# Value products of two attention steps in one block behind the scores of the even step, with a ring of 12 tiles of exponentials

## The reference

```python
q = (h @ Wq.T + bq).reshape(B, S, nh, hd)      # nh = 16, hd = 16, S = 2048
k = (h @ Wk.T + bk).reshape(B, S, nh, hd)
v = (h @ Wv.T + bv).reshape(B, S, nh, hd)
scores = jnp.einsum('bqhd,bkhd->bhqk', q, k) * scale
scores = jnp.where(causal, scores, jnp.finfo(scores.dtype).min)
attn = jax.nn.softmax(scores, axis=-1)
o = jnp.einsum('bhqk,bkhd->bqhd', attn, v).reshape(B, S, H)
return o @ Wo.T + bo
```

## Time and profile before

| what | value |
|---|---|
| median of 3 runs | 1266.43 us |
| profiled execution | 1264.95 us |
| its span | 1263.2 us |
| TensorE busy | 1106.1 us, 88% |
| VectorE busy | 705.4 us, 56% |
| ScalarE busy | 562.9 us, 45% |
| GpSimd busy | 110.1 us, 9% |
| exponentials L955 | 298.0 us, 640 of them |
| value products L894 | 158.2 us, 1280 records |

### The profile page before, as it was taken

The page is one execution under the profiler, slowest core; times in us unless marked ns, Lnnn a source line. Parts: engine busy times, 40 slices in busy tenths (PEclk is TensorE's granted clock), DMA queues, the critical chain, the costliest instruction groups (busy, mean ns, idle before and its releaser), DMA issues. The chain is left out here.

```text
span 1263.2 us, 19302 instructions
## 1 busy us (share of the span) xinstructions
PE 1106.1 (88%) x6480; PEld 719.7 (57%) x6480; DVE 705.4 (56%) x1604; ACT 562.9 (45%) x1102; POOL 110.1 (9%) x409
## 2 busy tenths in 40 slices
PE   3289999999968267888999999999966999999998
PEld 2178888888856022333333333333226888888886
DVE  7923333334367375776988888888516233333333
ACT  6422222222247024665577777777762232223222
POOL 0000000000000112332211111111121000000000
PEclk9999999999989558999999999999987999999999
DMA  5000000000027402112111101110000000000000
GB/s 172 1 1 1 1 1 1 0 0 0 0 65 181 105 23 61 50 50 70 27 44 47 43 24 36 40 47 2 1 13 1 1 1 17 1 17 0 17 0 17
DMA packets 69243, 37.24 MB, mean 29 GB/s; under 512 B 47409, under 2 KB 63025, under 8 KB 69169
## 3 DMA queue, kind: packets, MB, share of 16 engines
q1 hardware_dynamic: 69168, 36.32, 10.7%
HBM read 25.63 MB, written 10.49 MB: 29 GB/s over the span
## 5 line engine op out<-in xcount | busy, mean ns | idle before, releaser
L955 ACT ACTIVATE attn_prob<-psum 128x512 f32<-128x512 f32 (+3 forms) x640 | 298.0, 541 | 157.8 <-PE psum L858 157.0
L294 PE MATMUL psum<-ffn_xt,all_w_hi 128*128 128x512 f32 x1024 | 325.5, 399 | 4.9 <-DVE ffn_xt L375 4.9
L978 DVE TENSOR_REDUCE attn_part_max<-psum 128x1 f32<-128x512 f32 x384 | 242.2, 684 | 61.5 <-PE psum L870 60.1
L381 DVE TENSOR_TENSOR ffn_inner<-ffn_act_out,ffn_inner 128x512 fp32r<-128x512 f32 x128 | 88.6, 692 | 331.4 <-ACT ffn_inner L345 331.4
L870 PE MATMUL psum<-attn_k_st,attn_q_st 96*128 96x512 bf16 (+3 forms) x640 | 222.7, 366 | 50.2 <-DMA attn_vals<-v_rows 30.9
L353 ACT ACTIVATE ffn_act_out<-psum 128x512 f32<-128x512 f32 x128 | 76.5, 598 | 370.9 <-PE psum L294 370.8
L858 PE MATMUL psum<-attn_q_st,attn_k_st 99*128 99x512 bf16 (+3 forms) x640 | 219.9, 359 | 9.3 <-ACT attn_prob L955 5.2
L294 PEld LDWEIGHTS psum<-ffn_xt,all_w_hi 128*128 128x128 f32 x1024 | 185.1, 190 | 43.5 <-issue 5.7
L308 PE MATMUL psum<-all_w_hi,ffn_inner 128*128 128x256 f32 x1024 | 202.9, 281 | 4.1 <-DVE ffn_inner L381 4.1
L294 PE MATMUL psum<-ffn_xt,all_w_lo 128*128 128x512 f32 x512 | 203.5, 398 | 0.0
L308 PEld LDWEIGHTS psum<-all_w_hi,ffn_inner 128*128 128x128 f32 x1024 | 165.3, 188 | 10.8 <-DVE ffn_inner L381 5.7
(11 more groups left out here) (97 smaller groups left out, 666.0 us busy)
## 6 DMA issues: line engine op xcount, KB each, us to landing
qk_parts<-qkv_parts SPq DMA_DIRECT2D x16, 384.0 KB, 2.6
attn_q_st<-qk_parts SPq DMA_DIRECT2D x32, 96.0 KB
attn_k_st<-qk_parts SPq DMA_DIRECT2D x16, 192.0 KB
all_x<-in_L_attn_h SPq DMA_DIRECT2D x4, 512.0 KB, 7.5
v_rows<-qkv_rows_v SPq DMA_DIRECT2D x16, 128.0 KB, 3.4
attn_q_st<-qk_parts SPq DMA_DIRECT2D x32, 64.0 KB
attn_k_st<-qk_parts SPq DMA_DIRECT2D x32, 64.0 KB
attn_k_st<-qk_parts SPq DMA_DIRECT2D x16, 128.0 KB
```

The costliest lines, as they stand in the source:

```text
L294: last = nc.tensor.matmul(psum[:, 2 * m + q % 2, :], w_part[a][:, 3 * g + m, pl, o:o + P], xt[:, k, c, pl, :], start=(n == 0), stop=(n == 5))
L381: nc.vector.tensor_tensor(inner[:, 1, u, :], act_out[:, u, :], as_f32(inner[:, 0, u, :]), ALU.subtract).then_inc(s["inner_lo"], 1)
L955: nc.scalar.activation(prob[:, n % PRING, at:BT], psum[:, S0 + n % SBANKS, at:BT], ACT.Exp).then_inc(s["exp"], 1)
L978: nc.vector.tensor_reduce(to, psum[:, bank, :], AX.X, ALU.max).then_inc(s["max_read"], 1)
```

## The change

The value products of steps d - 2 and d - 1 are issued together behind the scores of an even step d; behind an odd step there are none. At the end the products of the last two steps follow. The ring of exponentials has 12 tiles, three steps, instead of 8, and ScalarE waits for the products of step d - 3 where it waited for those of step d - 2.

```diff
-PRING = 8
+PRING = 12
...
                             for g in turned(d):
                                 turn_max(g)
-                            if d >= 1:
+                            if d >= 2 and d % 2 == 0:
+                                weigh(d - 2)
                                 weigh(d - 1)
+                        weigh(NS - 2)
                         weigh(NS - 1)
                         gather(NG_A - 1)
...
                         for d, (g, kb) in enumerate(steps):
-                            if d >= 2:
-                                act.wait_ge(s["weighted"], d - 1)
+                            if d >= 3:
+                                act.wait_ge(s["weighted"], d - 2)
```

## The result

| | before | after |
|---|---|---|
| median | 1265.20 us (4 runs) | 1284.16 us (4 runs, 1282.05 to 1287.15) |
| profiled execution | 1264.95 us | 1284.92 us |
| span | 1263.2 us | 1283.2 us |

The ratio of after to before is 1.0152, 95% interval 1.0122 to 1.0182: 19 us slower. The forecast was 1280 us in a range of 1268 to 1291. In the changed source the lines from L926 on lie two lower: the exponentials are L957, the reads of the maxima L980 and L983, the copies L938 and L944. L858, L870 and L894 keep their numbers.

The account below looks back on a forecast made before the run. Three engines were taken as nearly level, held together by three score and three maximum banks. Terms 13.0 + 0.9 + 2 - 2 + 0 = +13.9 us on 1264.95 gave 1278.9, stated as 1280 us, range 1268 to 1291.

Parts of the forecast that it names:

- the cycle: Repeating 14 steps of query blocks 2 and 3 for a pair of heads: from 38.96 to 40.8 us.
- The saving at the joint: Two value runs in a row on TensorE: a pair costs 0.24 us less than two single runs.
- The starved readers: VectorE and ScalarE late once a pair: +1.86 us a cycle, +13.0 us over steps 49 to 146; chance 0.67.
- the last twelve: Steps 148 to 159, without maxima: two or three full pairs of 5.23 against 4.90 us, +0.9 us.
- Steps 12 to 35: Waits for masks shrink by 3.4 us, starvation adds 1.2: together -2 us, bounds -4 and +3.
- the wait for the masks: Steps 12 to 35: value products wait 1.0 us for POOL four times; 0.15 us remains of each, -3.4 us.
- Steps 37 to 48 and 1 to 6: Six maxima a step in steps 36 to 48: +2 us, bounds 0 and +4; first twelve steps: 0, bounds -1 and +1.
- a DMA that is waited for can swallow part of it: Steps 36 to 48: a DMA wait ending the first group can hide some of the +2.4 us starvation; no size given.
- A: Rival: readers catch up, each pair gives back 0.24 us on TensorE: 1245.5 us; chance 0.08.
- B: Rival: the slower reads and the saving cancel, within 0.5% of before, 1266 us; chance 0.09.
- C: Rival: the second value run hides nothing, 2.00 us a pair, 11 us more, 1291 us; chance 0.13.
- D: Rival: pairs don't run together, the second run waits for its step's last exponentials; above 1291 us; chance 0.03.

Follow-up runs that it names:

- ring alone: Kernel before with the ring of 12 tiles and ScalarE's looser wait, without the pairing: 1264.48 us, ratio 1.0001.
- mix: Kernel before with the larger ring, only products of even steps 8 to 33 and from 148 on issued one step late: 1263.08 us, ratio 0.9989.
- pair_covered: Changed kernel with products of steps 4 and 36 left behind the scores of steps 5 and 37: 1281.16 us, ratio 1.0123 to the kernel before.
- the pair kernel with both short reads: Changed kernel, VectorE reading every second column of maxima, ScalarE making exponentials of half of each tile's columns: 1237.25 us, ratio 0.9777.

## Why the prediction was right

The mechanism was the one forecast, readers starved once a pair, and the cycle was met. The sum was short, +13.9 us against 19 measured: two smaller terms, below, were mis-sized.

**The saving at the joint.** 0.24 us a pair was taken from the second pass behind the first. Shown: three kinds of pair give 0.24 with short reads, and a pair's value products take 1.85 us to the next score, with the passes at 0, 0.45, 0.88 and 1.31 as costed. Not foreseen was that pairs 2 and 5, with the transpose, save nothing even with quick readers. This trace contradicts the rule of the Trainium skill ("TensorE: Matmul & The Clock Gate", Part 3, what overlaps and what doesn't) for column groups: the loads of the second run, on the same rows, go at 0.45 and 0.88 us inside the running block. By the rule the pair was to cost 2.00 us.

**The starved readers.** The seven pairs were costed at 6.71, 5.54, 5.37, 6.71, 5.70, 5.53 and 5.26 us and took 6.64, 5.73, 5.30, 6.63, 5.89, 5.45 and 5.18; both sums are 40.82. That the sums agree to the last digit is luck: the pairs held by VectorE were costed 0.07 to 0.08 us too long, the two with ScalarE's copy 0.19 too short. The reads follow one another as read off, but the first starts 0.65 us after the first score (782.47 less 781.82) and not 0.72; the earlier trace rows shows one of the later starts. There the next exponential starts 0.43 us after the copy begins (784.24 to 784.67), not 0.26. That banks and reads are the cause in the cycle is shown from three sides: shorter reads turn its loss into a gain, a bank fewer brings pair and single together, and a stop in two halves gives back 0.53 us of 1.86, as reckoned. Over steps 49 to 146 the loss was 13.5 us (13.0 expected), 13.1 against the ring alone, and in the last twelve 1.0 (0.9).

**Steps 12 to 35.** Expected -2, measured -0.6. The wait for the masks went nearly as said, from 4.1 us in all to 1.3 (the same four), here in the kernel after:

```profile
527.30 0.63 PE L894 MATMUL psum<-attn_prob,attn_vals 128*32 128x256 f32 x8 [0.34 <-POOL attn_prob L831]
```

The rest of that stretch was not taken apart; steps 13 to 34 take 66.8 us before, 66.2 in the changed kernel, and 65.9 with single runs of which every second one is late (mix).

**Steps 37 to 48 and 1 to 6.** Mis-sized: +2 and 0 expected, +4.6 and +1.1 measured. The step that failed is "a DMA that is waited for can swallow part of it". It was the other way round: the wait already hid a run of products, and the change moved it out. pair_covered shows 1.0 us of it at step 38. In steps 5 and 6 together it is 14.1 us in the changed kernel, 13.0 in pair_covered and 12.1 to 12.8 before, with the ring alone and in mix, which fits but is within the scatter. The other terms of the +4.6 are these. The profiled kernel before happened to run step 38 at the higher clock; with the ring alone steps 37 to 48 take 50.1 us, not 49.2, so that the pairing costs 3.7 there. Step 44 takes 6.86 us, where pair_covered has 5.66: the granted clock of the stretch from 604.0 to 622.3 was 0.91 in the kernel after, and the loads of its value products came 0.76 and 0.85 us apart instead of 0.45 and 0.43. Whether the change brought this drop on is not shown. pair_covered, with neither, is 1.7 us above the ring alone; that is left for the starvation with six maxima a step, sized at 2.4 without the DMA.

**The rivals.** A (TensorE's saving decides) is what happens in the cycle once both readers are quick, with 1.2 us a cycle where seven times 0.24 would be 1.7. B did not come about, C neither (1.85 us a pair, not 2.00), nor D: the value products of both steps, sixteen records, stand in one block. One sign was misjudged: TensorE's busy share in the cycle fell to 97% (39.41 of 40.82), not 93, since the modelled ends of matmuls (0.39 us where the next can start after 0.22) cover a part of each gap.

## What to carry to other kernels

Where a producer feeds readers through a ring of n buffers, a stop of the producer is free up to what n reads last, less the way there and back; beyond that every reader's queue shifts, and a saving inside the stop must be larger than the shift. As an estimate from this kernel's rows: three reads of 0.60 us, less the 0.31 us from the last maximum to the stop, 0.23 from the first score to the first maximum and 0.42 from there to its read, leave 0.84 us. A stop of 1.0 us is just over that, one of 1.85 a full microsecond; with two banks 0.24 us are left. So work out, before fusing two stops, the time at which the last item of the longer run gets its buffer. And before moving work to a later place, look whether it now stands in front of a wait that hides it.

## What the runs showed of the hardware

Reading every second column of a PSUM tile of 512 (256 elements) takes VectorE 0.42 us instead of 0.68, and where tiles are waiting such reads follow each other every 0.33 us (four in 1.42 us, in the pair kernel with both short reads) instead of every 0.60:

```profile
598.14 1.42 DVE L980 TENSOR_REDUCE attn_part_max<-psum 128x1 f32<-128x256 f32 x4 [1.26 <-PE psum L870]
```

At the full granted clock a run of four fp32 matmuls of 512 columns in four column groups takes its second pass 0.45 us after the first, and every further pass, of the next run too, 0.43 us later; the weight loads of a pass go while the pass before is running. After a wait of 3.4 us for a DMA TensorE's next score took 0.39 us in one execution and 0.61 in another (before and ring alone, step 38), so a single trace doesn't tell what such a wait costs.
